# TensorE's waits at the first product's start, and the place of a transpose: one core, a fused FFN, scan and FFN block

## What is computed

```
x = x + 0.5 * ffn(layernorm(x))
x = x + ssm(layernorm(x))
x = x + 0.5 * ffn(layernorm(x))

ffn(x):  vecs[a, r] = A[a, r, :] . x            64 experts of rank 16: a 1024 x 1024 product
         the 4 experts with the largest norm of vecs are chosen (routes = 1/4 each, else 0)
         v = sum over the chosen of vecs         (rank 16)
         out = W x + bias + sum over the chosen of B[a] v
ssm(x):  xz = W_xproj x  ->  delta_r (128), B (16), C (16)
         delta = softplus(W_dt delta_r + b_dt)
         h[t] = exp(delta A) h[t-1] + delta B x;  y[t] = sum over 16 states of h C;  out = y + D x
```

## Time and profile before

| | |
|---|---|
| median of 3 runs | 2816.26 us (2815.76 to 2824.55) |
| profiled execution | 2817.88 us, span 2816.1 us |
| PE busy | 2600.7 us, 92% of the span |
| PEld | 1177.0 us, 42% |
| DVE | 2221.5 us, 79% |
| ACT | 1497.5 us, 53% |
| POOL | 2349.3 us, 83% |
| granted TensorE clock, mean | 0.985 |

### The profile page before, as it was taken

How to read it: one execution, slowest core, us unless ns; L and a number is a source line. 1 busy time by engine, 2 the same in 40 slices (tenths; PEclk the granted TensorE clock), 3 DMA queues, 4 the chain that set the end, 5 groups by cost and what they waited for, 6 DMA issues and landing times.

```text
span 2816.1 us, 39802 instructions
## 1 busy us (share of the span) xinstructions
PE 2600.7 (92%) x13597; PEld 1177.0 (42%) x13664; DVE 2221.5 (79%) x2933; ACT 1497.5 (53%) x3363; POOL 2349.3 (83%) x703
## 2 busy tenths in 40 slices
PE   4988999999999999999999999999999998889999
PEld 1444444444344443444444434444344443444444
DVE  8447888888788887888878878788788887888843
ACT  5346666665555645556455555565555554655521
POOL 2138889989899898998999999999899999989910
PEclk8999999999999999999999999999999999999999
DMA  5144434544354443544544445444455434454321
GB/s 218 48 116 136 142 118 135 163 144 138 108 159 143 133 138 109 159 144 128 143 138 132 144 138 160 133 127 131 145 156 157 143 117 138 131 147 139 92 63 53
DMA packets 303520, 373.50 MB, mean 133 GB/s; under 512 B 148435, under 2 KB 220243, under 8 KB 303318
## 3 DMA queue, kind: packets, MB, share of 16 engines
q1 hardware_dynamic: 286422, 337.40, 40.2%
q10 hardware_dynamic: 16896, 33.56, 4.0%
HBM read 234.05 MB, written 103.29 MB: 120 GB/s over the span
## 4 chain that ended last, share of the span: by engine, by line
PE 24%; DVE 18%; ACT 5%; DMA 5%; DVEq 4%; issue 4%; SPq 1%; ACTq 1%; POOL 1%; POOLq 0%
DVE mreg L1147 10%; PE pv L554 8%; PE po L554 5%; PE pv L558 4%; PE po L558 3%; ACT pA L934 2%; PE py L721 2%; DMA delta_scratch<-mreg 2%; DVE pv L1108 1%; DVE sel L1105 1%; DVEq L1113 1%; DMA mreg<-xnT_scratch 1%; DVEq L1107 1%; DMA xin<-x_scratch 1%; DVE xin L1071 1%
## 5 line engine op out<-in xcount | busy, mean ns | idle before, releaser
L522 POOL TENSOR_TENSOR mreg<-mreg 128x2048 f32<-128x2048 f32 x256 | 1161.6, 4538 | 48.8 <-ACT hst L920 48.7
L1147 DVE TENSOR_TENSOR_SCAN mreg<-pA,hst,mreg 128x512 f32<-128x512 f32 (+1 forms) x1024 | 1043.8, 1066 | 103.0 <-ACT pA L934 72.9
L512 POOL TENSOR_TENSOR mreg<-mreg 128x1024 f32<-128x1024 f32 x340 | 795.4, 2364 | 234.1 <-DMA mreg<-delta_scratch 229.9
L934 ACT ACTIVATE pA<-mreg,nA 128x512 f32<-128x512 f32 (+1 forms) x1280 | 738.3, 596 | 452.6 <-DVE mreg L1147 403.3
L554 PE MATMUL pv<-wA,xT 128*128 128x512 f16 x2016 | 463.8, 382 | 52.3 <-ACT xT L841 41.7
L554 PE MATMUL po<-wB,uT 128*128 128x512 f16 x2016 | 470.4, 380 | 10.2 <-DVE xin L1071 7.2
L554 PE MATMUL po<-wW,xT 128*128 128x512 f16 x2016 | 470.9, 381 | 3.6 <-issue 0.2
L506 POOL TENSOR_TENSOR mreg<-mreg 128x2048 f32<-128x2048 f32 x86 | 390.0, 4535 | 2.0 <-issue 2.0
L554 PEld LDWEIGHTS pv<-wA,xT 128*128 128x128 f16 x2016 | 191.8, 98 | 335.7 <-ACT xT L841 90.2
L554 PEld LDWEIGHTS po<-wB,uT 128*128 128x128 f16 x2016 | 191.8, 98 | 273.3 <-issue 47.0
L554 PEld LDWEIGHTS po<-wW,xT 128*128 128x128 f16 x2016 | 196.0, 98 | 238.3 <-issue 24.8
(11 more groups left out here) (132 smaller groups left out, 2376.0 us busy)
## 6 DMA issues: line engine op xcount, KB each, us to landing
mreg<-delta_scratch SPq DMA_DIRECT2D x256, 512.0 KB, 5.9
delta_scratch<-mreg ACTq DMA_DIRECT2D x128, 256.0 KB
xin<-x SPq DMA_DIRECT2D x32, 512.0 KB, 3.6
x_scratch<-xin SPq DMA_DIRECT2D x32, 512.0 KB, 6.1
xnT_scratch<-auxs SPq DMA_DIRECT2D x32, 512.0 KB, 2.9
mreg<-xnT_scratch SPq DMA_DIRECT2D x64, 256.0 KB, 6.7
yT_scratch<-mreg SPq DMA_DIRECT2D x64, 256.0 KB, 2.5
uT<-yT_scratch SPq DMA_DIRECT2D x32, 512.0 KB, 4.5
```

The lines of the kernel that those rows point to most:

```text
L512: pool.tensor_tensor(h[:, half * n:half * n + n, :], u, b.broadcast_to([P, n, c.width]), ALU.mult).then_inc(s_bm, 1)
L522: pool.tensor_tensor(h, h, by_c, ALU.mult).then_inc(s_cm, 1)
L934: last = nc.scalar.activation(dst[:, part, :], src[:, part, :], ACT.Exp, scale=nA[:, m:m + 1])
L1147: last = V.tensor_tensor_scan(h, split(pA[:, i % 2, :], c)[:, part, :], h, before, ALU.mult, ALU.add)
```

## The change

Three edits, all on TensorE's queue; no instruction but waits is added or removed.

- `experts`, first half of the columns: third 0 waits for the first high copy (and as before for the first low part), third 1 for the second high copy, third 2 for the second low part.
- The last four transposes of y move from right behind the first four to behind `states(a, 3)` and `base(a, 1, 1)`, that is eight matmuls later and, where the plan puts a group sum there, behind that sum.
- The waits for `s_nc` and `s_ya` ahead of `routed(a, 0, 0)` go. `scan_products` keeps its own.

```diff
             def experts(b, nb, third):
+                if nb == 0 and third < 2:
+                    pe.wait_ge(s_xhi, b.u * 2 + 1 + third)
                 if nb == 0 and third != 1:
-                    pe.wait_ge(s_xhi, b.u * 2 + 2)
                     pe.wait_ge(s_xlo, b.u * 2 + (1 if third == 0 else 2))
                 last = product(pv[:, nb, :], xT, wA, nb, third, True, True)
...
                     y_blocks(y, 0)
+                states(a, 3)
+                base(a, 1, 1)
                 if y:
                     y_blocks(y, 1)
-                states(a, 3)
-                base(a, 1, 1)
                 states(a, 4)
                 base(a, 1, 2)
                 states(a, 5)
                 if late:
                     scan_products(a, late, y)
-                if late:
-                    pe.wait_ge(s_nc, late.w * 2 + 2)
-                if y:
-                    pe.wait_ge(s_ya, y.v * 2 + 2)
                 routed(a, 0, 0)
```

## The result

| | before | after |
|---|---|---|
| median of 20 runs | 2817.34 us (2811.14 to 2824.55) | 2830.51 us (2818.97 to 2836.39) |
| profiled execution | 2817.88 us | 2835.22 us |
| granted clock, mean | 0.985 | 0.980 |

The ratio is 1.0043 (95% interval 1.0032 to 1.0054), which is 12.1 us more, 9 to 15. I had forecast 10 us less. The profiled execution of after lies near the top of its runs: it is 17.3 us longer than before's, so stages are read from it, but amounts from the ratios.

What follows compares the result with a forecast made beforehand. It took the chain through VectorE and ScalarE as the bound, TensorE only in the last units; -19.8 + 5.5 + 3.6 = -10.7 us from 2816.26 gave some 2806 us, range 2802 to 2810, with bounds and rivals 2792 to 2822.

Steps and rivals of the forecast that it cites:

- Edit 1, -19.8 us: Experts' start: eighteen units start 1.07 us earlier on the mean, two others give 0.55 together; 19.8 us gained, bounds 0 and 19.8.
- nine give nothing ... an earlier start only lengthens that wait: Experts: nine of 29 units gain 0; in eight the second low part comes late, in one TensorE itself.
- the clock's term: TensorE's half clock after idle time at the experts: taken as 0, bounds 5.1 us of gain and 7 of loss.
- Edit 2, SP's queue, +5.5 us: Later transposes delay the scan's spreads in units 55, 47 and 30: 3.5, 1.5 and 0.5 us lost, bounds 0 and 8.1.
- Three units run straight through: Only in units 30, 47 and 55 does SP issue the spreads with no later wait to absorb the delay; 5.5 us lost.
- Edit 2, the last three units, +3.6 us: Units 60 to 62: the routed operand lands later while TensorE is the bound; 3.6 us lost, bounds 3 and 5.
- Edit 2, the middle, 0: Middle units: the wait for y's gather becomes one for the DMA; 0, bounds 27.5 us of gain, 11.5 of loss.
- Edit 3, 0: The two waits dropped ahead of the routed product: the operand's landing, then the normed row replace them; 0, upper bound 7.2 us.
- The four signs of a right prediction: Second-copy wait from 41.7 to some 20 us, y's gather wait nearly gone, `uT` DMA wait appears, GpSimd's 9.2 to some 12.
- two signs of a wrong one: Wait for the normed row stays at 52 us, or VectorE's scan waits for GpSimd grow by over 10 us.
- The start's gain is taken back: Next unit's GpSimd and scan DMA waits absorb the experts' gain: three quarters gone 2820 us, half gone 2815; chance 0.25.
- SP's queue decides: Delayed transposes hold up spreads in most units, price 46 us: 2842 us with all, 2827 with two thirds; chance 0.12.

Runs made afterwards that it cites:

- edit 2 alone: Only y's last four transposes moved behind the group sum and eight matmuls, against the kernel before; ratio 1.0056, +15.7 us.
- edit 1 alone: Only the waits of the experts' three thirds split in the first half of the columns, against the kernel before; ratio 0.9962, -10.7 us.

## Why the prediction was wrong, point by point

- **Edit 1, -19.8 us: most of the gain came, and what the early start costs elsewhere was taken as nothing.** The step that failed is "nine give nothing ... an earlier start only lengthens that wait", and with it the clock's term, taken as 0. In the double stages the 1.1 us weren't neutral: two waits with 3.6 us of matmuls between them became a short and a longer one, and the half-clock time behind the low part in six of them went from 10.1 to some 26 us, worth 7 to 8 us (58.7 and 59.1 against 51.4), in the profile. That is the bound of 7 us of loss, which I wrote down and weighted with 0.10. The 22 stages behind one tile gave 16.0 to 17.1 us in three profiles (10.6 to 13.0 in those where the low part goes first). Part of that is the clock too: these stages held 17.1 us at half clock before and 13.6, 10.3 and 6.8 in the three, which is worth 1.7 to 5.2 us, so the start itself gave some 11 to 15 of the 19.8. Stages 22, 30, 54 and 55 kept 1.1 us each, 15, 23 and 31 only 0.1 to 0.5. Net -10.7.
- **Edit 2, SP's queue, +5.5 us: right place, too few units, and the clock left out.** Of the forecast's three units, stage 48 measured +1.9 (1.5 forecast), unit 30 nothing (0.5). Stage 56 measured +3.6 (3.5 forecast) in one profile and +5.4 to +5.9 in three, because the sum's longer wait can bring the half clock on the base product ahead of the transposes; that the profile of edit 2 alone hit the forecast is luck in part. The step that failed is "Three units run straight through": I had looked only for L360, for which GpSimd waits. L353 alone also stands behind the transposes, in units 17, 25 and 49. In two of them ScalarE had already waited for it (5.32 us in unit 17, 2.18 in unit 25), in unit 49 it waits 1.97 us only with edit 2; 4.7 us in stages 18, 26 and 50. The row on which I leaned against it, SP waiting for the scan's sums, tells of L394, and L353 was issued ahead of that.
- **Edit 2, the last three units, +3.6 us**: right to the tenth.
- **Edit 2, the middle, 0**: right outside of L353's units. TensorE's wait for the gather turned into one for the landing (3.0 to 38.5 us) and bought nothing.
- **Edit 3, 0**: right, within the 4 us that its interval leaves.
- **The signs.** The four signs of a right prediction all appeared (no wait of the experts for the second copy is left in the list, third 2's wait grew, y's wait is gone, the landing's wait came with GpSimd's 11.65 us), and the kernel was slower all the same: they showed that the steps were carried out, not what they are worth. Of the two signs of a wrong one, the first appeared as well: the wait for the normed row stayed (52.2 and 51.4). I had read it as "then the middle counts after all", but edit 2 alone is 15.7 us slower, so that rival falls, and the sign was no sign: the time went into the wait for the landing instead. The second, VectorE's scans waiting over 10 us more for GpSimd, did not appear (13.5 us before, 15.5 after), although SP's queue did decide what edit 2 costs: it reached the chain through ScalarE, whose wait for the spreads grew by 12.5 us.
- **The rivals.** "The start's gain is taken back" has half of it gone for edit 1, as measured, but by the wrong mechanism: what was taken back lay for the most part in the double stages, by the clock. Its round trip "of fixed length" isn't one here: the loads of L390 took 3.0 to 8.6 us to land before. "SP's queue decides" is the closest: of edit 2's 15.7 us some 12 lie outside the last three units, a quarter of its 46 us, in few units and not in most. The measured 2830.51 us lies outside the 2792 to 2822 that the bounds and rivals were to carry; near it is only this rival's 2827 with two thirds of the delay, and that is not how it came about.
- **Sum.** 19.8 to 10.7 is 9.1 us, 9.1 to 15.7 is 6.6: together most of the 22.8 between -10.7 and +12.1. The other 7 lie within the intervals of the single edits; the trace doesn't settle them. The whole change had the most half-clock time of all (75.1 us; edit 1 alone 51.2, edit 2 alone 41.0), but a kernel without edit 1 had 68.3.

## What to carry to other kernels

An earlier release of TensorE is worth something only if the next wait in its stream is not fixed by something else. If it is, the idle time is pushed together into one long wait, which here cost more than the two short ones, through the clock. So look for what fixes the later wait (here a wait for a DMA, written ahead of the low part) and move that first. When an instruction that releases a DMA queue is moved, list every transfer behind it, unit by unit, with the engine that already waits for each: a consumer that waits for it already before the change can pass on the whole delay, as in unit 25, and the same holds for transfers moved ahead, which must themselves be ready. A profile is one execution: where it is the shortest or longest run of its kernel, read places from it and amounts from the runs. Filling the idle time with work that changes nothing is a cheap test of whether the clock is the reason, even if it isn't the cure.

## What the runs showed of the hardware that I had not expected

- Idle time ahead of one group of matmuls was not free even though its end was fixed by another engine. With the low part as late (236.0 and 233.3 us from the stages' starts in sum), 46.1 us were needed behind it with the gap filled and 59.1 without. The same wait doesn't always bring the half clock: behind 2.21 us ahead of the sum in unit 55 it came after the whole change and not with edit 2 alone.
- A 256 KB store and three 512 KB spreads issued just ahead of two DMA transposes in the same queue came with 6.07 us of issuing for the transposes and left TensorE 4.98 us idle. One spread ahead cost nothing that showed where it was ready early, and 3.7 us a stage where the transposes had to wait behind it (units 40 and 56).
- The load of 256 KB by L390 took from 2.8 to 9.0 us to land in one execution, and the double stages, which wait for it, differed by some us from profile to profile even where no edit touched them.
